# Probabilities turned by DMA and a kernel listed by slots: a float32-exact macaron block on one Trainium2 core

## What is computed

```python
x = L0_attn_x                                   # (16, 256, 256)
x = x + 0.5 * ffn(layernorm(x))
x = x + attn(layernorm(x))
x = x + 0.5 * ffn(layernorm(x))

def ffn(x):                                     # wu, wg, wd: ternary_quant of the weights
    return (silu(x @ wu.T) * (x @ wg.T)) @ wd.T
def attn(x):                                    # 16 heads of 16, rope on q and k
    scores = einsum('bqhd,bkhd->bhqk', q, k) / 4 + causal
    return einsum('bhqk,bkhd->bqhd', softmax(scores), v).reshape(B, S, E) @ wo
```

## Time and profile before

| what | value |
|---|---|
| median of 3 runs | 887.43 us (884.81 to 891.82) |
| the profiled execution, its own time | 886.57 us |
| its span (first to last instruction) | 884.8 us |
| mean granted TensorE clock | 0.951 of full speed |
| PE busy | 708.4 us, 80% |
| DVE busy | 709.8 us, 80% |
| ACT busy | 620.1 us, 70% |
| POOL busy | 557.4 us, 63% |

### The profile page before, as it was taken

How to read it: one execution, slowest core, us unless ns; L and a number is a source line. 1 busy time by engine, 2 the same in 40 slices (tenths; PEclk the granted TensorE clock), 3 DMA queues, 4 the chain that set the end, 5 groups by cost and what they waited for, 6 DMA issues and landing times.

```text
span 884.8 us, 18797 instructions
## 1 busy us (share of the span) xinstructions
PE 708.4 (80%) x6976; PEld 584.6 (66%) x6976; DVE 709.8 (80%) x1591; ACT 620.1 (70%) x1365; POOL 557.4 (63%) x568
## 2 busy tenths in 40 slices
PE   0537578888888979898988888897979898767756
PEld 0325366777777868677777777786868777655544
DVE  2753486989998898988898999899898889777663
ACT  2104387878878788878887887878787788767642
POOL 2026685676768676767777676867676767744232
PEclk9968797999999999999999999999999999989798
DMA  8300312030303040302113030303040211213000
GB/s 317 119 1 1 72 29 45 13 66 9 73 13 73 14 72 13 72 14 48 39 21 65 1 73 14 72 14 73 14 72 14 55 31 31 55 29 57 1 13 13
DMA packets 110297, 40.20 MB, mean 45 GB/s; under 512 B 100992, under 2 KB 109440, under 8 KB 109696
## 3 DMA queue, kind: packets, MB, share of 16 engines
q1 hardware_dynamic: 109632, 36.71, 20.0%
q10 hardware_dynamic: 576, 2.29, 0.7%
HBM read 9.63 MB, written 4.19 MB: 16 GB/s over the span
## 4 chain that ended last, share of the span: by engine, by line
ACT 30%; PE 28%; DVE 19%; POOL 12%; issue 9%; DMA 1%; DVEq 0%; POOLq 0%; SPq 0%; ACTq 0%
PE misc_ps L386 7%; ACT prob L639 5%; ACT prob_h L630 5%; ACT tanh_b L648 5%; ACT prob L641 4%; PE pv_ps L435 4%; PE up_ps L386 3%; PE probt_ps L453 3%; POOL hid_l L1027 3%; DVE hid L934 3%; PE misc_ps L500 3%; ACT prob_t L634 3%; DVE silu_b L923 3%; PE score_ps L403 2%; POOL k_row L334 2%
## 5 line engine op out<-in xcount | busy, mean ns | idle before, releaser
L1027 POOL TENSOR_TENSOR hid_l<-hid,hid_h 128x512 f16<-128x512 f32 x128 | 148.5, 1161 | 225.9 <-ACT hid_h L654 210.9
L630 ACT ACTIVATE prob_h<-probt_ps 128x384 f16<-128x384 f32 x256 | 127.5, 498 | 76.5 <-PE probt_ps L453 76.2
L639 ACT ACTIVATE prob<-score_ps,exp_bias,exp_scale 128x256 f32<-128x256 f32 x256 | 147.2, 575 | 2.3 <-DVE exp_bias L874 1.2
L453 PE MATMUL probt_ps<-ident_f,prob 128*128 128x128 f32 x768 | 133.0, 283 | 13.8 <-ACT prob_t L634 13.8
L386 PE MATMUL up_ps<-xt_hi,tern_up 128*128 128x256 f16 x512 | 127.4, 286 | 20.2 <-DVE tern_up L708 13.1
L1020 POOL TENSOR_TENSOR prob_l<-prob_t,prob_h 128x384 f16<-128x384 f32 x128 | 118.1, 923 | 37.0 <-ACT prob_t L634 36.8
L386 PE MATMUL down_ps<-tern_down,hid_h 128*128 128x256 f16 x512 | 121.0, 276 | 19.3 <-POOL hid_l L1027 19.2
L386 PE MATMUL up_ps<-xt_lo,tern_up 128*128 128x256 f16 x512 | 127.4, 286 | 0.0
L386 PE MATMUL gate_ps<-xt_hi,tern_gate 128*128 128x256 f16 x512 | 123.9, 280 | 1.8 <-DVE tern_gate L708 1.8
L386 PE MATMUL gate_ps<-xt_lo,tern_gate 128*128 128x256 f16 x512 | 123.1, 279 | 0.0
L641 ACT ACTIVATE prob<-score_ps,exp_bias,exp_scale 128x128 f32<-128x128 f32 x256 | 121.2, 473 | 0.0
(11 more groups left out here) (101 smaller groups left out, 1868.4 us busy)
## 6 DMA issues: line engine op xcount, KB each, us to landing
xs<-x SPq DMA_DIRECT2D x16, 256.0 KB, 2.8
out<-xs SPq DMA_DIRECT2D x16, 256.0 KB, 2.1
raw_gate<-w_gate_t ACTq DMA_DIRECT2D x1, 1024.0 KB, 7.6
raw_up<-w_up_t SPq DMA_DIRECT2D x1, 1024.0 KB, 7.7
raw_down<-w_down_t SPq DMA_DIRECT2D x1, 1024.0 KB, 10.4
raw_w<-wqkvo ACTq DMA_DIRECT2D x1, 1024.0 KB, 12.5
cos<-rope_cos SPq DMA_DIRECT2D x1, 512.0 KB, 13.6
sin<-rope_sin SPq DMA_DIRECT2D x1, 512.0 KB, 14.4
```

The costliest lines, as they stand in the source:

```text
L453: mm = pe.transpose(probt_ps[:, n * P:(n + 1) * P], prob[:, pair % 2, j, col * P:(col + 1) * P], ident_f[:, :])
L630: act.activation(prob_h[:, pair % 2, j, :], probt_ps[:, 0:384], ACT.Copy).then_inc(prob_h_done, 1)
L639: act.activation(prob[:, s % 2, j, 0:256], score_ps[:, j, 0:256], ACT.Exp, bias=exp_bias[:, j:j + 1], scale=exp_scale[:, :])
L1027: pool.tensor_tensor(hid_l[:, s % 2, :, :].rearrange("p m n -> p (m n)"), hid[:, s % 2, :], hid_h[:, s % 2, :, :].rearrange("p m n -> p (m ...
```

## The change

1. The probabilities are no longer turned by TensorE. ACT casts the unturned float32 tile of both heads at once (`prob_hi`, 128 x 768, SBUF to SBUF), POOL takes the low part of both heads at once (`prob_lo`, 128 x 768), and SP issues one DMA transpose of both parts (128 x 1536 float16, twelve blocks of 128 x 128) for each pair of heads (`turn_probs`). `prob_lo_1` on DVE, ACT's `prob_t` copy and the `probt_ps` bank go away. `product_v` comes three slots behind the scores (`PV_LAG`), not two. The freed bank gives `up_ps` a second buffer, and `tanh_b` has two.
2. The scores of two heads share their matmuls: four for each pair of heads instead of six, over as many columns (1280). `neg_max` lies in PSUM, so `exp_biases` reads PSUM.
3. `pv_scale` multiplies straight out of PSUM and `pv_add` adds the two halves afterwards, out of SBUF.
4. Steps are replaced by slots from -18 to 138. Pair n of heads has slot n. `plan_rounds` puts the first feed-forwards of batches 0 to 5 into slots -15 to 8, without a gap; that of batch b from 6 on starts at slot 8(b-6)+17, the second feed-forward of batch b at slot 8b+13. `xt_hi` and `xt_lo` of norm 1 have two buffers.
5. Each engine has one list for all slots. DVE's has `norm_var` behind `hidden`, POOL's has `norm_power` first, both for the norms of `STATS_AT[g]`, that is in the same slot g. POOL still does the rotary embedding; `qk_rows` is gone, ACT copies q and k into `rope_c` and `rope_mul` works in place.

In the diff, the last `slot` is POOL's; `norm_power` waits for `var_done[k]` of the same slot. `PE_OTHER`, `ACT_OTHER`, `ACT_EXTRA`, `DVE_OTHER`, `DVE_EXTRA` and the eight lists of the old `POOL_SLOT` go too.

```diff
-PE_SLOT = ["scores", "product_v", "misc_a", "transpose_0", "up", "gate", "transpose_1", "misc_b",
-           "down"]
...
+PAIRS = NBATCH * SLOTS
+PV_LAG = 3
+FIRST_FFN = -15
+AHEAD = 6
+def plan_rounds():
+    plan = [(FIRST_FFN + ROUNDS * b + r, 1, b, r) for b in range(AHEAD) for r in range(ROUNDS)]
+    plan += [(SLOTS * (b - AHEAD) + 17 + r, 1, b, r) for b in range(AHEAD, NBATCH) for r in range(ROUNDS)]
+    plan += [(SLOTS * b + 13 + r, 2, b, r) for b in range(NBATCH) for r in range(ROUNDS)]
+    return sorted(plan)
+FFN_ADD = {FFN_START[f, b] + ROUNDS + 1: (f, b) for f, b in FFN_ORDER}
+OF_BATCH = [("norm2", -8, "b"), ("qk0", -7, "b"), ("qk1", -6, "a"), ("v", -5, "b"), ("attn_t", 10, "b"),
+            ("out_proj", 11, "a"), ("norm3", 12, "b")]
+MISC = sorted([(SLOTS * b + at, place, what, b) for what, at, place in OF_BATCH for b in range(NBATCH)] +
+              [(FFN_START[1, b] - 1, "a", "norm1", b) for b in range(NBATCH)])
+STATS_LEAD = {1: 2, 2: 2, 3: 1}
+STATS_AT = {}
+for _slot, _place, _what, _b in MISC:
+    if _what.startswith("norm"):
+        _k = int(_what[-1])
+        STATS_AT.setdefault(_slot - STATS_LEAD[_k], []).append((_k, _b))
+ROPE_MUL = {-6: 0, -5: 1}
+ROPE_ADD = {-5: 0, -4: 1}
+ROPE_HI = {-4: 0, -3: 1}
+ROW_LO = {-3: 0, -2: 1}
+PE_SLOT = ["scores", "product_v", "misc_a", "up", "gate", "misc_b", "down"]
+ACT_SLOT = ["prob_hi", "misc_a", "tanh", "exps_0", "exps_1", "rope_hi", "misc_b", "hidden_hi"]
+DVE_SLOT = ["row_max", "exp_bias", "pv_inverse", "ffn_added", "pv_scale", "misc_a", "norm_stats", "pv_add", "silu",
+            "norm_mean", "hidden", "norm_var", "norm_apply", "misc_b"]
+POOL_SLOT = ["norm_power", "rope_add", "rope_mul", "prob_lo", "row_lo", "norm_apply", "hidden_lo"]
...
+            def turn_probs(n):
+                sp.wait_ge(prob_l_done, n + 1)
+                if n >= 2:
+                    sp.wait_ge(pv_done, n - 1)
+                sp.dma_start_transpose(prob_t[:, n % 2, :, :, :].rearrange("p a c q -> p (a c) q"),
+                                       prob_hl[:, n % 2, :, :].rearrange("p a k -> p (a k)")
+                                       ).then_inc(prob_turned[n % 2], 16)
+            for g in range(FIRST_SLOT, LAST_SLOT + 1):
+                n = pair_at(g - 1)
+                if n is not None:
+                    turn_probs(n)
+                turned = batch_event(g, ROW_LO)
+                if turned:
+                    turn_rows(*turned)
...
+            def exps(n, tile):
+                act.wait_ge(bias_done, n + 1)
+                if tile and n >= 2:
+                    act.wait_ge(prob_l_done, n - 1)
...
+            def prob_hi(n):
+                act.wait_ge(exp_done[0], n + 1)
+                act.wait_ge(exp_done[1], n + 1)
+                if n >= 2:
+                    act.wait_ge(prob_turned[n % 2], 16 * (n // 2))
+                act.activation(prob_hl[:, n % 2, 0, :], prob[:, n % 2, :], ACT.Copy).then_inc(prob_h_done, 1)
...
+            def prob_lo(n):
+                pool.wait_ge(prob_h_done, n + 1)
+                pool.tensor_tensor(prob_hl[:, n % 2, 1, :], prob[:, n % 2, :], prob_hl[:, n % 2, 0, :], ALU.subtract
+                                   ).then_inc(prob_l_done, 1)
...
+            def slot(g):
+                for what in POOL_SLOT:
+                    if what == "norm_power":
+                        for k, b in STATS_AT.get(g, []):
+                            norm_power(k, b)
+                    elif what == "norm_apply":
+                        for k, b in STATS_AT.get(g - 1, []):
+                            if k != 3:
+                                norm_apply(k, b)
...
+                    elif what == "prob_lo" and pair_at(g - 1) is not None:
+                        prob_lo(g - 1)
+                    elif what == "row_lo" and batch_event(g, ROW_LO):
+                        row_lo(*batch_event(g, ROW_LO))
+                    elif what == "hidden_lo" and g in ROUND_AT:
+                        hidden_lo(ROUND_AT[g][0])
```

More of the change, by code:

```diff
@@ L95 @@
[L95 to L117, removed]
-    return 0 <= b < NBATCH
-def misc_before(t, name):
-    index = [m[0] for m in MISC].index(name)
-    done = sum(live(u - lag) for u in range(FIRST_STEP, t) for _, _, _, lag in MISC)
-    return done + sum(live(t - lag) for _, _, _, lag in MISC[:index])
@@ L158, in run_steps @@
-def run_steps(engine, body, before={}):
-    for t in range(FIRST_STEP, LAST_STEP + 1):
-        if t in before:
-            before[t]()
-        body(Step(t))
+PAIRS = NBATCH * SLOTS
[7 more added lines that the diff above has]
+    return sorted(plan)
@@ new lines, in through, with added, pair_at, batch_event @@
+def through(what, b):
+    return MISC_INDEX[what, b] + 1
+def added(f, b):
+    return FFN_ORDER.index((f, b)) + 1
+def pair_at(slot):
+    return slot if 0 <= slot < PAIRS else None
+def batch_event(slot, table):
+    for at, value in table.items():
+        b, rest = divmod(slot - at, SLOTS)
+        if rest == 0 and 0 <= b < NBATCH:
+            return b, value
+    return None
+def run_slots(engine_slot, before={}):
+    for g in range(FIRST_SLOT, LAST_SLOT + 1):
+        if g in before:
+            before[g]()
+        engine_slot(g)
@@ new lines, in misc @@
+                mm.then_inc(misc_written, 1)
+            def slot(g):
+                for what in PE_SLOT:
+                    if what == "scores" and pair_at(g) is not None:
+                        scores(g)
+                    elif what == "product_v" and pair_at(g - PV_LAG) is not None:
+                        product_v(g - PV_LAG)
+                    elif what.startswith("misc"):
+                        for name, b in MISC_AT.get((g, what[-1]), []):
+                            misc(name, b)
+                    elif what == "up" and g in ROUND_AT:
+                        up(*ROUND_AT[g])
+                    elif what == "gate" and g in ROUND_AT:
+                        gate(*ROUND_AT[g])
+                    elif what == "down" and g - 1 in ROUND_AT:
+                        down(*ROUND_AT[g - 1])
@@ L560, in _ @@
             pe.wait_ge(ident_loaded, 16)
-            run_steps(pe, step, before={1: lambda: pe.wait_ge(casts_done, 3)})
+            run_slots(slot, before={0: lambda: pe.wait_ge(casts_done, 3)})
         @block.scalar
@@ L673, in _ @@
             set_up_loads()
             sum_weights()
-            run_steps(act, step, before={0: lambda: act.wait_ge(scales_done, 4)})
+            run_slots(slot, before={FIRST_FFN: lambda: act.wait_ge(scales_done, 4)})
         @block.vector
@@ new lines, in norm_mean, with norm_var @@
+            def norm_mean(k, b):
+                dve.wait_ge(stats_done[k], 2 * (b + 1))
+                for tile in range(NT):
+                    dve.bn_aggr(mv[k][:, tile, :], stats[k][:, tile, :]).then_inc(mean_done[k], 1)
+            def norm_var(k, b):
+                dve.wait_ge(mean_done[k], 2 * (b + 1))
+                dve.tensor_scalar(var_s[k][:, :, None], mv[k][:, :, 1:2], X_SCALE ** -2, LN_EPS * X_SCALE ** -2,
+                                  ALU.mult, ALU.add).then_inc(var_done[k], 1)
```

764 lines of the change are left out of this document (302 added, 462 removed), and 6 rows, old and new, of the table ACT_OTHER.

## The result

The changed kernel takes 996.66 us (median of 4 runs, 994.82 to 997.58), the kernel before beside it 887.93 us: 1.122 times as long, 95% interval 1.117 to 1.127. It is 109 us slower. The forecast was 948 us with a range to 988: the direction was right, the size too small by 49 us.

What follows compares the result with a forecast made beforehand. No engine was taken as full; the order in which four in-order engines hand a slot on sets the pace. Stages of 103, 79, 570, 157 and 38 us sum to 947, given as about 948 us, range 885 to 988.

Steps and rivals of the forecast that it cites:

- p=3: Slot whose number modulo 8 is 3, where norm 3 has its statistics: POOL stands about 4.4 us for the variance.
- p=6: Slot whose number modulo 8 is 6, where norms 1 and 2 have their statistics: POOL stands about 4.4 us again.
- slots 97 to 127: Late slots with half the rounds and no norm 1: two periods of 43 us, then 39 and 32, 157 us.
- p0: Slot whose number is a multiple of 8: walked through at 9.5 us, PE's norm transposes waiting for POOL's `norm_apply`.
- to the first scores: Start of the kernel: weights split at 61.7 us, ten rounds of 3.1 us, 10 us of POOL work; 103 us.
- B: Rival for the whole time: POOL's waits are absorbed, period 43.5 us, total 835 us; chance 0.12.
- C: Rival: turning by DMA is late, landing taken as 6 us, `prob_hi` stands in two slots of eight; 990 us, chance 0.08.
- D: Rival: the clock stays low for most of a period, 3.5 us instead of 1; 974 us, chance 0.07.
- E: Rival: both waits half as long, period 48 to 49.5 us, total 885 to 897, no change; chance 0.08.
- slots 0 to 12: First slots with scores: eight without norm 3 (51), p0 with one norm (7), four without rounds (21); 79 us.
- the tail: After the last exponential: 34.5 us as before plus 3.5 for the DMA between `prob_lo` and `product_v`; 38 us.
- the shared port: DVE and POOL's SBUF port: DVE pays, POOL does not, nothing in the sum; if POOL lost too, near 970 us.

Runs made afterwards that it cites:

- e1: The changed kernel with POOL's `norm_power` moved behind `norm_apply`, just ahead of `hidden_lo`; 900.34 us, 1.017 times the kernel before.
- e9: The kernel of e6 with no first feed-forwards run ahead, that of every batch b starting at slot 8b-15; 898.31 us, 1.012 times the kernel before.
- e6: The kernel of e5 with DVE's `norm_apply` of norm 3 put ahead of `silu`; 897.7 us, 1.010 times the kernel before.
- e5: The changed kernel with POOL's list as `prob_lo`, `norm_apply`, rotary work, `row_lo`, `norm_power`, `hidden_lo`; 899.76 us, 1.012 times the kernel before.
- e3: The changed kernel with `norm_power` just ahead of `hidden_lo` and `prob_lo` over only 384 of 768 columns, the rest zero; 885.53 us, 0.998 times the kernel before.
- e11: The kernel of e6 with norm 3 applied by POOL, and norm 1's statistics, power and apply one slot earlier; 888.99 us, 1.0007 times the kernel before.

## Why the prediction was right in direction and too small

**Right: the wait and what stands behind it.** The idle time of `rstd` was forecast at 100 to 140 us and is 130.0; POOL's busy time at 640 to 660 and is 647.3; the period of eight steady slots at 54.2 and is 54.6 (mean of the eight periods from pair 24 to 88). The experiments make this cause and not company: the wait moved away gives back 96 us, the wait put into the kernel before costs 39.

**The size of the single wait was not right.** Forecast were 4.4 us at p=3 and again at p=6; measured are 3.86 and 2.93, 69.6 us in all in slots 13 to 96. The total of 130.0 is met because the start, the slots 97 to 127 and the last norm add the rest. In the check of the period, 40.3 of work, 8.8 and 3.2 of waits and 1 of gaps, the work is 40.2, but the waits for the variance are 6.8 and those for ACT's cast before `hidden_lo` 7.4: two errors that nearly cancel.

**Right in sum, uneven inside.** Slot by slot, from the first exponential of one pair to that of the next, in the period from 488.2 us on: p0 12.5 (forecast 9.5), p1 to p3 16.1 (17.1), p4 7.9 (8.6), p5 7.5 (5.9), p6 4.5 (5.0), p7 6.1 (7.1), in sum 54.6 (53.2 and 1 for the clock). Two slots were under-counted by 4.6 us, the others over-counted by 3.2; that the sum fits so well is partly luck. p5 comes behind PE's stand for norm 3. p0 has the two stands shown above, 5.24 us for `hidden_lo` and 2.36 for the rows of q and k; the second is in no term of the forecast, which asked of the turning only whether the probabilities behind `turn_rows` are late, and not the rows themselves. The wait that the forecast did name for p0, PE's norm transposes for `norm_apply`, does not show in the steady slots.

**Right: the prices.** `prob_lo` 1.64 forecast, 1.642 measured; `prob_hi` 0.87 and 0.846; the landing 3.8 and 3.7. `exp_bias` fell from 458 to 222 ns. `pv_scale` fell from 543 to 290, and `pv_add`, which has moved behind it, takes 286 where it took 278: with `exp_bias` 0.48 us a slot are gained, and 0.45 were forecast. The mean clock is 0.836, under 0.95 as forecast.

**Failed: the term "slots 97 to 127", 157 us against 179.** This and the next are the steps that put the forecast too low. The term was scaled from the kernel before ("43 us a period while there is rotary work", since such eight slots take 44 there) and not walked, though norms 2 and 3 still end in those slots. The waits of the kernel after, from 773 to 952 us:

```profile
POOL rstd L872 <- DVE var_s L744: 26.8, 6, 8.0
...
PE misc_ps L454 <- DVE xhat L750: 20.7, 4, 5.3
ACT prob L580 <- POOL prob_hl L916: 16.1, 5, 4.5
```

The same trio as in the steady part, and e1, without the wait at POOL's head, takes 15.5 us less there (176.4 to 160.9). The first periods there take 50.0 and 48.4 us, where 43 were forecast. Half the feed-forward work shortens a period, 54.6 us before, by 5 to 6 us and not by 11, while the waits stay.

**Failed: the term "to the first scores", 103 us against 120.** It took over from the kernel before that the weights are split at 61.7 us, and priced ten rounds at 3.1 us each and POOL's norm and rotary work at 10 in all. In the kernel after DVE splits the weights later (start us, duration us):

```profile
62.75 3.64 DVE L721 SCALAR_TENSOR_TENSOR w_lo<-raw_w,w_mul,w_hi 128x512 f16<-128x512 f32 x4
```

They are split at 66.4 us, 4.7 later, and the ten rounds with POOL's work then take 53.7 us instead of 41. In e9, with fewer rounds ahead, they are split at 55.5. After 66.4 us PE stands six times for more than 1 us, 15.7 us in all: 7.3 before `down`, 6.0 for an applied norm, 2.4 for the rows of q and k. Of the 22 us that the changed kernel needs more than e9 to its first `exp_bias`, 13.5 are the rounds run ahead (e9 against e6), 2.2 DVE's later apply (e5 against e6, no more than two executions may differ by) and 6 the power at the head (e1 against the changed kernel).

**Small: slots 0 to 12 and the tail**, 3 and 4 us.

**The rivals.** B, the absorbed wait, had 0.12: its 43.5 us a period was never reached, not even by e3 with its lighter POOL (47.75). C, late turning: the probabilities land after 3.7 us and not 6, ACT waits 26.8 us for them, and what is late besides is not them but the rows of q and k, 37.2 us of PE; how much of that is on the path no run shows. D, the clock: a part of the loss, not separated in its cost. Behind PE's stand of 5.24 us the granted clock is 0.50 from 491.6 to 500.2 us, and 1.00 again from 500.7. E had waits half as long; they are three quarters of the forecast, and the period did not shrink with them.

On the shared port the row had said that DVE pays and POOL does not. It holds: in the changed kernel DVE's two `xhat` take 2.74 us beside a `prob_lo` of 1.64, its usual length, and POOL's operations of that stretch are at most 0.05 us above their mean. The Trainium skill (SBUF — State Buffer, Who interferes with whom) calls the pair of ports an exclusive lock; the numbers agree: DVE is held until a POOL operation has ended (last section), and none shows a POOL operation blocked for an `xhat`.

The range was too narrow at the top: its bounds took in mechanisms (the clock, the DMA) but not the two stage terms that had been taken over from the kernel before; the bounds of the first, 93 to 113, were left by 7 us. With the 22 and 17 us that they lacked the sum in the span would have been 986, against 994. A slip besides: 947 and the two steps of 1.8 and 0.9 give 950, not 948.

## What to carry to other kernels

In an in-order queue a wait costs more than its own idle time, since all that is queued behind it is late; put an operation that waits for the same slot's result behind everything that does not need it. Price every stage by walking its waits, the start and the end as well: a stage scaled by its amount of work came out 12 to 14% short here, twice. And engines with a quarter of their time to spare promise nothing while a slot is handed from one to the next: with 133 us of work less on DVE, 56 less on ACT and 121 more on POOL the best version that leaves nothing out, e11, takes the time of before.
